# SyncE's first loads after a loop are moved in front of the loop block's exit

## The reference

```
xn  = layernorm(x)
x1  = x + graph_attention(xn over the edges) + linear_attention(xn)
h   = layernorm(x1)
expert of a node = argmax of softmax(h @ gate_w + gate_b), 8 experts,
                   each takes at most C = 977 nodes in order of node number
y   = relu(h @ w1[e] + b1[e]) @ w2[e] + b2[e], times the gate's probability
out = x1 + y (0 for a node that found its expert full)
```

## Time and profile before

| | |
|---|---|
| runs | 3516.04, 3519.21, 3537.9 us |
| the profiled execution | 3527.52 us, its span 3526.3 us, 1.2 us around it |
| busy: TensorE, VectorE, ScalarE, GpSimd | 66%, 68%, 30%, 60% |
| edge loop's block | to about 2999.7 us |
| norm, gate and routing | 2999.7 to 3132 us |
| experts | 3132 to 3526 us |
| granted TensorE clock | 0.50 from 2990 to 3140 us, 1.00 from 3150 us |
| SyncE at the join in line 1430 | 832.3 us of waiting |

### The profile page before, as it was taken

The page is one execution under the profiler, slowest core; times in us unless marked ns, Lnnn a source line. Parts: engine busy times, 40 slices in busy tenths (PEclk is TensorE's granted clock), DMA queues, the critical chain, the costliest instruction groups (busy, mean ns, idle before and its releaser), DMA issues. The chain is left out here.

```text
span 3526.3 us, 39395 instructions
## 1 busy us (share of the span) xinstructions
PE 2310.5 (66%) x9498; PEld 1811.7 (51%) x9499; DVE 2381.8 (68%) x3245; ACT 1070.8 (30%) x4461; POOL 2110.5 (60%) x2220
## 2 busy tenths in 40 slices
PE   3839236667666666666777776555555653659998
PEld 1527125555455555555555555344444432549998
DVE  2314247777677767778887877677888974636665
ACT  1513015555454554652111111100010100435443
POOL 5050566665666666666666666666666665447776
PEclk7858668888888888878888878778787876569999
DMA  4533466666666666666777777666666662823341
GB/s 131 205 77 141 124 177 181 179 182 168 185 183 183 184 181 185 176 177 202 210 218 207 215 214 212 183 186 186 187 181 184 182 188 75 288 81 75 91 90 28
DMA packets 258265, 590.78 MB, mean 168 GB/s; under 512 B 49410, under 2 KB 135505, under 8 KB 257565
## 3 DMA queue, kind: packets, MB, share of 16 engines
q0 software_dynamic: 150480, 467.10, 48.2%
q1 hardware_dynamic: 97947, 109.47, 9.4%
q10 hardware_dynamic: 9296, 9.44, 0.8%
HBM read 519.05 MB, written 71.76 MB: 168 GB/s over the span
## 5 line engine op out<-in xcount | busy, mean ns | idle before, releaser
L959 POOL DMA_INDIRECT wide<-kv_d,arena x1099 | 1055.6, 961 | 588.7 <-issue 390.8
L1255 PE MATMUL ps<-wide,arena 128*128 128x264 f32 x2432 | 765.0, 475 | 373.3 <-issue 246.2
L1255 PEld LDWEIGHTS ps<-wide,arena 128*128 128x128 f32 x2432 | 567.8, 239 | 560.2 <-issue 295.2
L959 POOL DMA_INDIRECT arena<-kv_d,arena x539 | 516.9, 959 | 304.9 <-issue 189.1
L1359 DVE TENSOR_REDUCE arena<-arena 128x64 f32<-128x2048 f32 x229 | 523.5, 2286 | 7.9
L1356 DVE TENSOR_TENSOR arena<-wide,ps 128x2048 f32<-128x2048 f32 x153 | 349.4, 2283 | 256.1 <-ACT ps L1102 153.0
L1255 PE MATMUL ps<-arena 128*128 128x264 f32 x1216 | 382.1, 479 | 137.6 <-issue 74.3
L1255 PEld LDWEIGHTS ps<-arena 128*128 128x128 f32 x1216 | 288.6, 242 | 229.6 <-issue 93.9
L1392 DVE TENSOR_TENSOR wide<-wide,ps 128x2112 f32<-128x2112 f32 x152 | 356.8, 2347 | 16.7 <-ACT arena L1111 9.9
L134 PE MATMUL ps<-halves 128*128 128x256 f32 (+2 forms) x2304 | 361.4, 319 | 3.2 <-DVE halves L1625 1.6
L134 PEld LDWEIGHTS ps<-halves 128*128 128x128 f32 x2304 | 331.1, 192 | 31.0 <-POOL halves L1635 3.5
(11 more groups left out here) (321 smaller groups left out, 3290.6 us busy)
## 6 DMA issues: line engine op xcount, KB each, us to landing
wide<-kv_d,arena POOLq DMA_INDIRECT x1099
arena<-in_w SPq DMA_DIRECT2D x16, 1024.0 KB
kv_d<-wide SPq DMA_DIRECT2D x49, 260.0 KB
arena<-xn_d SPq DMA_DIRECT2D x98, 128.0 KB
arena<-kv_d,arena POOLq DMA_INDIRECT x539
hb_d<-arena SPq DMA_DIRECT2D x16, 516.0 KB, 4.4
q_d<-wide SPq DMA_DIRECT2D x49, 128.0 KB
xn_d<-arena SPq DMA_DIRECT2D x7, 896.0 KB, 8.1
```

The costliest lines, as they stand in the source:

```text
L959: e.indirect_dma_start(out=kvb[k][:, j, :], out_offset=None, in_=kv_d, in_offset=bass.IndirectOffsetOnAxis(ap=ixb[k][:, j:j + 1], axis=0)) ...
L1255: m = e.matmul(psE[(k + 1) % 3][:, 0:264], ident, kvb[b][:, j, 256:ROW], start=(j == 0), stop=(j == J - 1))
```

## The change

SyncE's part of the block now goes on. It waits until ScalarE, TensorE and VectorE have each counted up a new semaphore `e_end` at the end of their parts, issues the load of `w1[0]`, waits for `e_bs` and for all 49 writes of `at_d`, and issues the 15 loads of attention and base rows. Then it comes to the block's end. After the block these loads, their waits and `load_w(0, 0)` are gone, so SyncE's first instruction there is the write of group 0 to `out`. GpSimd adds nothing to `e_end`. The order and the work of the other engines are as before.

```
@@ SyncE's part of the block, at its end @@
+            e.wait_ge(e_end, 3)
+            s_we[0].inc(e.dma_start(w1r, kpart(w1[0])), 16)
+            for k in range(RING):
+                e.wait_ge(e_bs[k], 16 * (AUX + (k == RING - 1)))
+            e.wait_ge(s_ag.h, 16 * NT)
+            for grp in range(7):
+                n_ = 7 if grp < 6 else 6
+                c0, r0 = grp * 7, grp * 896
+                rows_of = lambda d, r, n: d[r:r + 128 * n, :].rearrange("(t p) d -> p t d", p=128)
+                s_x2[grp].inc(e.dma_start(XH[:, c0:c0 + 7, 0:256], rows_of(at_d, r0, 7)), 16)
+                t_x2[grp] = s_x2[grp].inc(e.dma_start(XH[:, c0:c0 + n_, 256:512], rows_of(base_d, r0 + 128, n_)), 16)
+            t_x2[6] = s_x2[6].inc(e.dma_start(XH[:, 48, 256:512], base_d[0:128, :]), 16)
@@ ScalarE's part, at its end @@
+            e.reg_add(g_, g_, RING)
+            e.wait_ge(e_ix, g_)
+            e.nop().then_inc(e_end, 1)
@@ after the block @@
-        for k in range(RING):
-            Y.wait_ge(e_bs[k], 16 * (AUX + (k == RING - 1)))
-        wait(Y, t_fin, t_ag)
-        for grp in range(7):
-            ... (the same 14 loads)
-        t_x2[6] = dma(Y, XH[:, 48, 256:512], base_d[0:128, :], s_x2[6])
...
-        wait(Y, t_fin)
-        load_w(0, 0)
```

More of the change, by code:

```diff
@@ L839, in gps_layer_kernel @@
         e_xw = [esem(f"xw{i}") for i in range(2)]
-        s_ag = sem("s_ag")
+        s_ag, e_end = sem("s_ag"), esem("end")
+        XH = R12[:, 0:NT * XW].rearrange("p (t w) -> p t w", w=XW)
+        w1r, w2r = r3(R0[:, 0:2048], 1024), r3(R0[:, 2048:4096], 256)
+        s_x2 = [sem(f"s_x2_{i}") for i in range(7)]
+        s_we = [sem("s_we0"), sem("s_we1")]
+        t_x2 = {}
         e_so, e_si, e_sa, e_sd, e_se, e_sl = [esem(n) for n in ("so", "si", "sa", "sd", "se", "sl")]
@@ L1427, in _ @@
             e.nop().then_inc(sv.h, 1)
+            e.nop().then_inc(e_end, 1)
         sv.n += 2
         loop.close()
-        t_fin = (sv, sv.n)
+        t_fin, t_first, t_sum = (sv, sv.n), (s_we[0], 16), {}
         s_ag.n = 16 * NT
         t_ag = (s_ag, s_ag.n)
-        XH = R12[:, 0:NT * XW].rearrange("p (t w) -> p t w", w=XW)
         hT = [r3(IDX[:, 512 + 256 * i:768 + 256 * i], 128) for i in range(3)]
@@ L1442, in gps_layer_kernel @@
         reset = R3[:, 3951:3951 + 456]
-        s_x2 = [sem(f"s_x2_{i}") for i in range(7)]
-        for k in range(RING):
-            Y.wait_ge(e_bs[k], 16 * (AUX + (k == RING - 1)))
-        wait(Y, t_fin, t_ag)
-        t_x2, t_sum = {}, {}
-        for grp in range(7):
[L1449 to L1453, removed]
-        t_x2[6] = dma(Y, XH[:, 48, 256:512], base_d[0:128, :], s_x2[6])
         wait(V, t_fin)
@@ L1598, in center_h @@
             t_h[u] = a(S.activation(XH[:, u, 256:512], XH[:, u, 0:256], ACT.Identity, bias=nms[b][:, i:i + 1], scale=rss[b][:, i:i + 1]))
-        w1r, w2r = r3(R0[:, 0:2048], 1024), r3(R0[:, 2048:4096], 256)
         b1_s = R0[:, 4096:4160]
@@ L1613, in gps_layer_kernel @@
         w1h, w1l = [r3(HL[:, 25344 + 2048 * i:25344 + 2048 * (i + 1)], 1024) for i in range(2)]
-        s_we = [sem("s_we0"), sem("s_we1")]
         t_l1, t_l2, t_xp, t_xc, t_y = {}, {}, {}, {}, {}
-        t_wl, t_ws = ({}, {}), ({}, {})
+        t_wl, t_ws = ({0: t_first}, {}), ({}, {})
         def load_w(e, i):
```

## The result

Nineteen runs of each kernel: 3522.62 us before, 3535.23 us after (medians), ratio 1.0036 with a 95% interval of 1.0022 to 1.005. That is 12.6 us more; 12 were forecast.

A forecast was written before the change was run, and what follows sets the result against it. SyncE's held issues were taken to bound the join, moving the first sum 19.7 us; the stall, lasting as long as GpSimd's scatters, leaves about 12 us. Median 3519.2 + 12 = 3531 us, range 3508 to 3547 us.

The forecast's parts named there:

- The join waits for SyncE, and SyncE for its own issues: Block's end: 15 row-load issues hold SyncE 33.27 us, all engines wait, VectorE's first sum starts 19.7 us later.
- Rival 2: Block's end: the join does not hold the others for SyncE; end 6 to 17 us earlier, about 3508 us; chance 0.08.
- rival 3: SyncE's queue: issues inside the block take 0.40 us each, join covered by GpSimd's DRAIN, about 3508 us; chance 0.04.
- The weights: SyncE's queue: the `w1[0]` load ahead of the row loads adds 1.2 us to their issues, bounds 0 and 3.0 us.
- SyncE's DRAIN does not wait for transfers: Block's end: SyncE's DRAIN costs nothing, taken from one 14 ns row; otherwise 6 to 8 us more.
- GpSimd's split falls into VectorE's lead: Behind the join: GpSimd splits `w1[0]` before the first slots are ready, so scatters start 6.9 us later, not 19.7.
- The run of scatters ends 9.5 us later: GpSimd's routing scatters, batches 1 to 3 at 1.29 us each: run ends at 3110.1 us instead of 3100.64 us.
- The stall lasts as long as the run of scatters: Tile chain, VectorE's 25.12 us wait: it ends 3.4 us after GpSimd's scatters, so 9.5 us later, and is 10 us shorter.
- The 2.5 us for tiles to be done behind the stall: Tile chain after VectorE's long wait: one or two tiles it let through come later, 1.2 us each, about 12 us in all.
- Rival 1: Tile chain: the whole shift stays, +19.7 us (3539), or SyncE's DRAIN waits for loads, 6 to 8 more (3546); chance 0.27.
- Rival 4: Tile chain: the stall goes away with the gap between batches 1 and 2; 3 us less, 3516 us; chance 0.16.

The follow-up runs named there:

- the third set: Runs on a chip of the other kind: kernel before 3522.3 us, all routing scatters held behind the last routing 3557.82 us, four loads plus weights with smaller first batch 3505.63 us.
- the second set: Kernels before and after run again beside each other on one chip: 3065.45 us before, 3077.7 us after, ratio 1.0036.

## Why the prediction was right, by its steps

- *The join waits for SyncE, and SyncE for its own issues*: right. Join forecast at 36.9, measured 38.0; the issues took 32.7 us. Rival 2 (the join does not count SyncE) and rival 3 (issues inside the block are short) are refuted by the order of the DRAINs and by the dose of zero, four, eight and fifteen loads. Three loads of 896 KB are short to issue, at 0.40 to 0.56 us, and the fourth is not. The section of the Trainium skill that I set against this, in "DMA: Bandwidth & Descriptors", is titled in full "Anatomy of one DMA — SWDGE (gpsimd) path": its 50 ns and its "a lot of descriptors" are said of DMAs that GpSimd issues, and I had applied them to SyncE's. So the runs neither bear it out nor refute it.
- *The weights*: mis-sized. I let them cost SyncE 1.2 us in its queue and the last attention scatter nothing, with 3.0 us as the bound. They delayed that scatter by 2.5 us and the queue behind it not at all (the fourth issue took 2.78 us for 3.41 us before). The two errors partly make up for each other: join 38.0 for 36.9, first sum 39.3 for 37.9.
- *SyncE's DRAIN does not wait for transfers*: right, 0.12 us.
- *GpSimd's split falls into VectorE's lead*: right, the first scatter is 9.6 us later with a sum that is 21.1 us later. I had 6.9 us. Of the difference 1.4 us is the later sum, 0.6 us stands between the sum and the slots, and 0.8 us between the slots and the scatter, which I had put at nothing. (The split takes 12.0 us by the earlier trace rows and not 12.2 us; it is hidden either way.)
- *The run of scatters ends 9.5 us later*: it was 13.6, a term that I had too small. The second batch starts at 95.7 for 92.9, as its slots come 2.0 us later than I had them and the scatter 0.8 us behind them; two long scatters of the first batch fall into the pause in front of it, 1.6 us for the 3.6 us that I had. Another 1.7 us is one long scatter of the second batch. VectorE's sums lengthen them, and I had no term for it: I priced every scatter at 1.29 us. That is the plain pace; the 45.26 us for 34 steps that I gave as its source make 1.33 us, as they hold one scatter of 2.24 us, and I did not ask why it was long.
- *The stall lasts as long as the run of scatters*: right. VectorE goes on 2.8 us behind the end of the run after, 3.5 us before. I let VectorE's long wait shrink by 10 us; it shrank by 5.2 us. The run ended 4.1 us later than I had it. The 2.5 us for tiles to be done behind the stall did not show: VectorE's wait ended 13.0 us later, 0.7 us less than the run's end. *Two errors of opposite sign*, of 4.1 and 3.2 us, meet here, and that the sum of 12 us came out is in part luck.
- *Rival 1, the whole shift stays*: no. 8 of 21 us come back. On the chips without the stall they come back too, by the slack that the tile chain has against GpSimd: the loss is 10.9 us there, for a reason that I had not priced for the kernel before, GpSimd's scatters being the bound. That my sum fits both kinds of chip is in part luck.
- *Rival 4*: the stall did not go away, the gap of 1.6 us between batches is too short for that or does not matter.

## What to carry to other kernels

An engine that comes to a join must have issued its DMAs, and a full queue holds it for the transfer time of what it issues: before you move loads ahead of a barrier, count how many the queue takes at once (here three, at 0.4 to 0.6 us; 2.5 us each from then on), and move only as many as can be issued while the barrier waits for something else anyway (here GpSimd's DRAIN, until 9.4 us). The early start was worth 16 us with four row loads and the weights behind them, and cost 11 to 12 with fifteen, on the chips without the stall. See also which transfer is under way when a moved one starts: the weights in front delayed the very scatter that the row loads waited for. And when a change shifts two engines against each other, look for instructions of theirs that slow each other down: here three sums of VectorE fell on GpSimd's scatters instead of one.

## What the runs showed that I had not expected

- The same kernel took 3062 to 3069 us on two chips and 3506 to 3539 us in two sets of runs elsewhere. The profiles differ in waits called remote: none on the chips with the shorter time; on the chip of the third set ScalarE has the most, and GpSimd, VectorE and TensorE have some. The largest two (us in all, times, longest):

```profile
ACT arena L1058 <- remote: 277.3, 32, 35.6
...
ACT arena L1028 <- remote: 218.4, 21, 38.0
```

  Between the profile of before in the second set and the first profile of before, the busy times of VectorE and GpSimd are the same within 0.4% (2374.0 and 2381.8 us, 2108.9 and 2110.5 us), and TensorE's is 2188.0 against 2310.5 us. So most of the 460 us is waiting. Why the chips differ stays open. The ratio of after to before is 1.0036 on both.
- GpSimd's DRAIN took 9.6 us on the one kind of chip and 23 to 24 us on the other, but was over 9.4 us behind the start of its last scatter on both: it began with the others' and lasted over the scatters still to be done.
- A routing scatter that meets one of VectorE's sums took 1.6 to 2.7 us instead of 1.0 us.
